# Softmax attention: score parts in two layers of 48 rows, four score banks, three single banks of maxima

## The reference, cut to what matters

```python
q, k, v = (proj(Wq), proj(Wk), proj(Wv))            # 16 heads of 16, of layernorm(x)
q, k = _apply_rope(q, k, cos, sin)
scores = jnp.einsum('bhqd,bhkd->bhqk', q, k) / jnp.sqrt(jnp.float32(dk))
attn = jax.nn.softmax(scores, axis=-1)
out = jnp.einsum('bhqk,bhkd->bhqd', attn, v)
out = out.transpose(0, 2, 1, 3).reshape(B, S, D)
return out @ Wo.T                                    # and x is added
```

## Time and profile before

| | |
|---|---|
| median of 3 runs | 2536.96 us (2531.14 to 2543.85) |
| the profiled execution | 2535.98 us, of which its span 2534.3 us |
| busy over the span | PE 94%, DVE 66%, ACT 52%, POOL 46% |
| the changed stage (`attention_mix`) | about 234 to 1102 us of the span |

### The profile page before, as it was taken

The page is one execution under the profiler, slowest core; times in us unless marked ns, Lnnn a source line. Parts: engine busy times, 40 slices in busy tenths (PEclk is TensorE's granted clock), DMA queues, the critical chain, the costliest instruction groups (busy, mean ns, idle before and its releaser), DMA issues. The chain is left out here.

```text
span 2534.3 us, 48428 instructions
## 1 busy us (share of the span) xinstructions
PE 2376.7 (94%) x14822; PEld 1280.9 (51%) x14822; DVE 1666.4 (66%) x3797; ACT 1328.7 (52%) x2742; POOL 1154.1 (46%) x1497
## 2 busy tenths in 40 slices
PE   8997999999999999979998996999999969998997
PEld 5663233333333333346656664566666646655765
DVE  6777888888888888547763333677777757764332
ACT  5666676667776676645433333455555525432322
POOL 7998111111111111124326775677777734325776
PEclk9998799999999999989998998999999989998999
DMA  6655433323232322136767884011111025685886
GB/s 190 218 188 164 122 87 96 93 88 100 76 106 80 104 84 84 34 96 211 262 225 202 226 210 81 14 39 39 35 39 37 18 72 186 203 299 166 230 221 109
DMA packets 286870, 325.20 MB, mean 128 GB/s; under 512 B 30496, under 2 KB 272368, under 8 KB 286704
## 3 DMA queue, kind: packets, MB, share of 16 engines
q1 hardware_dynamic: 252928, 274.22, 34.7%
q0 software_dynamic: 29184, 46.43, 9.0%
q10 hardware_dynamic: 4592, 2.47, 0.4%
HBM read 217.29 MB, written 105.19 MB: 127 GB/s over the span
## 5 line engine op out<-in xcount | busy, mean ns | idle before, releaser
L718 DVE TENSOR_REDUCE a_row_max<-a_ps_m 128x2 f32<-128x1024 f32 x512 | 607.6, 1219 | 85.0 <-PE a_ps_m L621 80.1
L778 ACT ACTIVATE a_probs<-a_ps_s 128x512 f32<-128x512 f32 x1024 | 536.9, 602 | 207.6 <-PE a_ps_s L649 207.3
L664 PE MATMUL a_ps_o<-a_probs,a_va 128*32 128x512 f32 x2048 | 274.1, 608 | 0.8 <-ACT a_o_sb L787 0.8
L1758 POOL TENSOR_TENSOR b_spread<-b_decay,held_own_sb 128x512 f32<-128x512 f32 x256 | 267.7, 1077 | 8.6 <-DVE b_weight L1819 8.6
L1819 DVE TENSOR_TENSOR b_weight<-b_ps_s,b_spread 128x512 f32<-128x512 f32 x256 | 163.7, 682 | 9.4 <-PE b_ps_s L1960 9.4
L649 PE MATMUL a_ps_s<-first_qs,first_ks 98*128 98x512 bf16 (+1 forms) x512 | 161.3, 396 | 3.5 <-DMA first_qs<-a_m_parts 3.5
L649 PE MATMUL a_ps_s<-second 98*128 98x512 bf16 (+1 forms) x512 | 156.9, 386 | 4.4 <-DMA second<-a_m_parts 2.4
L558 POOL CAST a_high<-a_row_max 128x32 bf16<-128x32 f32 x32 | 6.5, 204 | 316.8 <-DVE a_row_max L718 316.8
L599 POOL DMA_DIRECT2D x<-a_xo x32 | 24.2, 755 | 275.1 <-DVE a_xo L752 272.6
L317 PE MATMUL a_ps_qk<-a_w_qk,a_xnT 128*128 128x512 f32 x256 | 122.2, 600 | 0.0
L1568 DVE SCALAR_TENSOR_TENSOR m2e_h<-m2e_act_g,m2e_xg,m2e_ps_h 128x192 f32<-128x192 f32 x64 | 26.5, 415 | 138.1 <-ACT m2e_act_g L1497 138.1
(11 more groups left out here) (397 smaller groups left out, 5397.0 us busy)
## 6 DMA issues: line engine op xcount, KB each, us to landing
parts<-second SPq DMA_DIRECT2D x16, 1536.0 KB, 6.2
second<-parts SPq DMA_DIRECT2D x384, 64.0 KB, 2.2
rows<-m_early SPq DMA_DIRECT2D x32, 640.0 KB, 3.7
m_early<-x SPq DMA_DIRECT2D x31, 512.0 KB, 4.0
first_qs<-parts SPq DMA_DIRECT2D x192, 64.0 KB, 2.4
first_ks<-parts SPq DMA_DIRECT2D x192, 64.0 KB, 2.2
m_own<-in_L_ffn_w_gate_dram SPq DMA_DIRECT2D x24, 384.0 KB, 4.5
m_own<-in_L_ffn_w_up_dram SPq DMA_DIRECT2D x24, 384.0 KB, 5.2
```

The costliest lines, as they stand in the source:

```text
L664: last = nc.tensor.matmul(ps_o[VW * j:VW * (j + 1), :], va[n.u][:, t, (h0 + j) * VW:(h0 + j + 1) * VW], probs[:, group % 2, j, t, :], star ...
L718: nc.vector.tensor_reduce(row_max[:, n.k // 4 % 2, t, :, n.p % 4], m_bank(name, step)[:], AX.X, ALU.max).then_inc(m_drained, 1)
L778: nc.scalar.activation(probs[:, group % 2, j, t, :], s_bank(name, step)[:], ACT.Exp, scale=DK ** -0.5).then_inc(s_drained, 1)
L1758: nc.gpsimd.tensor_tensor(spread[:, n % 2, heads].rearrange("p h t c -> p (h t) c"), decay[:, n % 3, heads].rearrange("p h (t o) -> p (h t ...
```

## The change

The six blocks are no longer stacked in one contraction of 96 rows. `qs` and `ks` now hold two layers: layer 0 has blocks 0 to 2 (those of the maximum product) and layer 1 blocks 3 to 5 with the two rows of -1 and of the maximum behind them. In each layer e = 0 has the rows from 0 on and e = 1 those from 64 on (`EDGE`). A score is now two matmuls that add up in one bank, of 48 and of 50 rows, and those of e = 0 and 1 alternate, so that every score product has the shape of the maximum products. `scores(t)` makes both heads' scores of key tile t: four matmuls, two banks, and its wait is for both banks at once; it stands four times in a step instead of eight. `ps_m` becomes a ring of three single banks with a turn of its own for every product, and a TENSOR_REDUCE takes 512 columns, one head; `ps_s` becomes a ring of four banks. `exponentials(i)` now serves head i % 2 and tile i // 2. TensorE's order in a step is new: max0, scores 0, scores 1, max1, turn_output, mix (lag 8), turn_shift, max2, scores 2, scores 3, max3, turning, projection, mix (lag 7). ScalarE's order is not changed: `copy_output` is still third.

```diff
-ROW = ((0, 16, 32, 48, 64, 80), (64, 80, 96, 0, 16, 32))
+LAYERS = 2
+EDGE = 64
...
-                row = ROW[e][slot]
-                yield tile[row:row + 16, f * 8 + e:(f + 1) * 8:2, :], src[e]
+                row = EDGE * e + slot % MAX_SLOTS * 16
+                yield tile[row:row + 16, f * 4:(f + 1) * 4, slot // MAX_SLOTS, :], src[e]
...
-    M_RING, S_RING = 2, 3
-    M_ORDER = [("max0", 0, 1, 0), ("output", L_OTURN, 2, 1), ("shift", L_TURN, 4, 3), ("max1", 0, 1, 0), ("max2", 0, 1, 0), ("max3", 0, 1, 0),
-               ("out0", L_OUT[0], PAIRS, PAIRS - 1), ("out1", L_OUT[1], PAIRS, PAIRS - 1)]
+    M_RING, S_RING = 3, 4
+    M_ORDER = ([(f"max{i}", 0, 1, 0) for i in range(4)] + [("output", L_OTURN, 2, 1), ("shift", L_TURN, 4, 3)]
+               + [(f"max{i}", 0, 1, 0) for i in range(4, 8)] + [(f"out{q}", L_OUT[q], PAIRS, PAIRS - 1) for q in range(2)])
...
-        ps_m = [pb(f"ps_m{u}", [P, 2, S]) for u in range(M_RING)]
+        ps_m = [pb(f"ps_m{u}", [P, S]) for u in range(M_RING)]
...
-            nc.gpsimd.memset(ks[0][32:64, 1::2, :], -1.0).then_inc(rows_set[0], 1)
-            nc.gpsimd.memset(qs[0][32:64, 1::2, :], 0.0).then_inc(rows_set[0], 1)
-            nc.gpsimd.memset(ks[0][96:98, 0::2, :], -1.0).then_inc(rows_set[0], 1)
+            for e in range(2):
+                at = slice(EDGE * e + FILL_ROW, EDGE * (e + 1))
+                nc.gpsimd.memset(ks[0][at, :, 1, :], -1.0).then_inc(rows_set[0], 1)
...
-                    name = f"max{t}"
-                    wait(pe, m_drained, m_turn(name, step) + 1 - M_RING)
+                    names = [f"max{2 * t + e}" for e in range(2)]
+                    wait(pe, m_drained, m_turn(names[1], step) + 1 - M_RING)
                     for e in range(2):
-                        rows = slice(ROW[e][0], ROW[e][0] + MAX_SLOTS * DK)
-                        last = nc.tensor.matmul(m_bank(name, step)[:, e, :], qs[u][rows, 2 * n.p + e, t * P:(t + 1) * P], ks[u][rows, 2 * n.p + e, :],
-                                                start=True, stop=True)
-                    last.then_inc(m_filled, 1)
+                        rows = slice(EDGE * e, EDGE * e + PART_ROWS)
+                        nc.tensor.matmul(m_bank(names[e], step)[:], qs[u][rows, n.p, 0, t * P:(t + 1) * P], ks[u][rows, n.p, 0, :],
+                                         start=True, stop=True).then_inc(m_filled, 1)
...
-                    name = f"score{i}"
-                    wait(pe, s_drained, s_turn(name, step) + 1 - S_RING)
-                    h = 2 * n.p + e
-                    nc.tensor.matmul(s_bank(name, step)[:], ks[u][0:K_ALL[e], h, t * P:(t + 1) * P], qs[u][0:K_ALL[e], h, :],
-                                     start=True, stop=True).then_inc(s_filled, 1)
+                    names = [f"score{2 * t + e}" for e in range(2)]
+                    wait(pe, s_drained, s_turn(names[1], step) + 1 - S_RING)
+                    for layer, shift_rows in ((0, 0), (1, 2)):
+                        for e in range(2):
+                            rows = slice(EDGE * e, EDGE * e + PART_ROWS + shift_rows)
+                            last = nc.tensor.matmul(s_bank(names[e], step)[:], ks[u][rows, n.p, layer, t * P:(t + 1) * P], qs[u][rows, n.p, layer, :],
+                                                    start=layer == 0, stop=layer == 1)
+                            if layer == 1:
+                                last.then_inc(s_filled, 1)
...
-            walk_pairs(pe, [(0, max_products(0)), (L_S, scores(0)), (L_S, scores(1)), (L_OTURN, turn_output), (L_MIX + 1, mix_values(1)),
-                            (L_TURN, turn_shift), (0, max_products(1)), (L_S, scores(2)), (L_S, scores(3)), (0, max_products(2)), (L_S, scores(4)), (L_S, scores(5)), (L_MIX, mix_values(0)),
-                            (0, max_products(3)), (L_S, scores(6)), (L_S, scores(7)),
-                            (L_ATT[0], turn_att(0)), (L_ATT[1], turn_att(1)), (L_OUT[0], project(0)), (L_OUT[1], project(1))])
+            walk_pairs(pe, [(0, max_products(0)), (L_S, scores(0)), (L_S, scores(1)), (0, max_products(1)),
+                            (L_OTURN, turn_output), (L_MIX + 1, mix_values(1)), (L_TURN, turn_shift),
+                            (0, max_products(2)), (L_S, scores(2)), (L_S, scores(3)), (0, max_products(3)),
+                            (L_ATT[0], turn_att(0)), (L_ATT[1], turn_att(1)), (L_OUT[0], project(0)), (L_OUT[1], project(1)), (L_MIX, mix_values(0))])
...
-                    name = f"max{t}"
-                    dve.wait_ge(m_filled, m_turn(name, step) + 1)
-                    nc.vector.tensor_reduce(row_max[:, n.k // 4 % 2, t, :, n.p % 4], m_bank(name, step)[:], AX.X, ALU.max).then_inc(m_drained, 1)
+                    for e in range(2):
+                        name = f"max{2 * t + e}"
+                        dve.wait_ge(m_filled, m_turn(name, step) + 1)
+                        nc.vector.tensor_reduce(row_max[:, n.k // 4 % 2, t, e, n.p % 4:n.p % 4 + 1], m_bank(name, step)[:], AX.X, ALU.max).then_inc(m_drained, 1)
...
-                    group, j, t = n.k // 2, 2 * (n.k % 2) + i // QT, i % QT
+                    group, j, t = n.k // 2, 2 * (n.k % 2) + i % 2, i // 2
```

More of the change, by code:

```diff
@@ L384, in attention_mix @@
         woT = sb("woT", [P, 2, D])
-        fill = sb("fill", [P, 2])
+        fill = sb("fill", [P, 1])
         ident, wo_rows = const["ident_sb"], const["wo_rows"]
-        qs = [const["first_qs"], const["second"][:, 0:H * S].rearrange("p (h t) -> p h t", h=H)]
-        ks = [const["first_ks"], const["second"][:, H * S:].rearrange("p (h t) -> p h t", h=H)]
+        qs = [const["first_qs"], const["second"][:, 0:H * S].rearrange("p (g l t) -> p g l t", g=PAIRS, l=LAYERS)]
+        ks = [const["first_ks"], const["second"][:, H * S:].rearrange("p (g l t) -> p g l t", g=PAIRS, l=LAYERS)]
         vs = sb("vs", [P, QT, D])
@@ L536, in heads_of @@
                 return va[u][:].rearrange("p t (h w) -> p t h w", w=VW)
-            for k, value in enumerate((-1.0, 0.0)):
-                nc.gpsimd.memset(fill[:, k:k + 1], value).then_inc(fill_set, 1)
-            pool.wait_ge(fill_set, 2)
-            nc.gpsimd.memset(ks[0][32:64, 1::2, :], -1.0).then_inc(rows_set[0], 1)
-            nc.gpsimd.memset(qs[0][32:64, 1::2, :], 0.0).then_inc(rows_set[0], 1)
-            nc.gpsimd.memset(ks[0][96:98, 0::2, :], -1.0).then_inc(rows_set[0], 1)
-            pool.wait_ge(rows_set[0], 3)
+            nc.gpsimd.memset(fill[:], -1.0).then_inc(fill_set, 1)
+            pool.wait_ge(fill_set, 1)
+            for e in range(2):
+                at = slice(EDGE * e + FILL_ROW, EDGE * (e + 1))
+                nc.gpsimd.memset(ks[0][at, :, 1, :], -1.0).then_inc(rows_set[0], 1)
+            pool.wait_ge(rows_set[0], 2)
             for u in range(2):
@@ L632, in turn_shift, with scores @@
                 for t in range(QT):
-                    last = nc.tensor.transpose(bank[0:2 * HALF, 0, t * P:(t + 1) * P], high_low[:, t].rearrange("p e r g -> p (e r g)"), ident[:])
+                    last = nc.tensor.transpose(bank[0:2 * HALF, t * P:(t + 1) * P], high_low[:, t].rearrange("p e r g -> p (e r g)"), ident[:])
                 last.then_inc(m_filled, 1)
-            def scores(i):
+            def scores(t):
                 def stage(n, step):
-                    u, e, t = n.u, i // QT, i % QT
-                    if n.p % 4 == 0 and i == 0:
+                    u = n.u
+                    if n.p % 4 == 0 and t == 0:
                         f = n.p // 4
                         pe.wait_ge(rest_loaded[u][f], 16 * 4 * (len(Q_PARTS) - MAX_SLOTS) * (n.base + n.k // PERIOD + 1))
-                        pe.wait_ge(rows_set[u], 3)
+                        pe.wait_ge(rows_set[u], 2)
                         pe.wait_ge(w_copied, 1)
@@ L676, in turn_output @@
                 for t in range(QT):
-                    last = nc.tensor.transpose(bank[:, 0, t * P:(t + 1) * P], o_sb[:, group % 2, t * P:(t + 1) * P], ident[:])
+                    last = nc.tensor.transpose(bank[:, t * P:(t + 1) * P], o_sb[:, group % 2, t * P:(t + 1) * P], ident[:])
                 last.then_inc(m_filled, 1)
@@ L727, in copy_shift @@
                 wait(dve, m_odd_loaded[f], n.base * 64 + n.k // PAIRS * 32)
[L728 removed]
+                nc.vector.tensor_copy(m_parts[:, f, :], m_bank("shift", step)[0:2 * HALF, :]).then_inc(m_drained, 1)
             def normalise(n, step):
@@ L750, in stage @@
                     wait(dve, stored[q], n.base * 32 + n.k // PAIRS * 16)
-                    out = m_bank(f"out{q}", step)[:, 0, :].rearrange("p (t d) -> p t d", d=D)
+                    out = m_bank(f"out{q}", step)[:].rearrange("p (t d) -> p t d", d=D)
                     nc.vector.tensor_tensor(xo[:, q], out, xr[n.u][:, 2 * q:2 * q + 2, :], ALU.add).then_inc(m_drained, 1)
                 return stage
-            walk_pairs(dve, [(0, maxima(0)), (L_OTURN, normalise), (L_TURN, copy_shift), (0, maxima(1)), (0, maxima(2)), (0, maxima(3)),
```

(13 more changed lines are left out.)

29 lines of the change are left out of this document (13 added, 16 removed).

## The result

The changed kernel takes 2598.01 us (median of 4 runs, 2590.73 to 2602.92) against 2536.89 before: a ratio of 1.0239 (95% interval 1.0219 to 1.0260), slower. Forecast were 2577 and slower with a chance of 0.82; the time lies in the range, 21 us above the forecast. The span of the profiled execution grew by 59.4 us, from 2534.3 to 2593.7.

What follows compares the result with a forecast made beforehand. TensorE, busy 99 of 100 us at full clock, was taken as the bound. Odd steps +61, even steps -22 and the start +5 and -3 gave +41 on 2536.0: 2577 us, eight-in-ten range 2532 to 2625.

Steps and rivals of the forecast that it cites:

- The shape changes removed: TensorE: six of ten changes of shape a step go, sets 0.225 us apart; natural even step 4.90 us, 0.54 less.
- Rival 2: TensorE: side-by-side pairs lose 0.10 us each time; even steps 5.84, odd 7.35, total 2644 us; chance 0.07.
- The wait that comes in: Odd steps: the last scores(t) waits for exponential 3, queued behind the copy; stall 1.2 us, odd step 7.01 against 6.01.
- Rival 1: Odd steps: the wait for exponentials 2 and 3 does not bite; odd step 5.81, total 2504 us; chance 0.11.
- rival 4: Odd steps: half of the wait is hidden, 0.6 instead of 1.2 us; +4, total 2540 us; chance 0.06.
- Reductions: VectorE: 512-column reductions 0.61 us apart, 0.68 long; second M not before 1.16, so an even step is 4.96.
- Turning and projection: Steps 1 to 4: one more change of shape, 0.1 us each, between M and a mix; projection stays 1.83.
- The start: First steps at half clock: M pairs every 1.38 us instead of 1.12, +5; next four steps gain 0.8 each, -3.
- Rival 3: Attention stage: new pauses make the clock fall; 2603 us if one in four does, 2680 if all; chance 0.10.
- The sum: Whole kernel: odd steps +61, even steps -22, start +5 and -3; in all +41 us on 2536.0.
- The two weighed rules of the Trainium skill: VectorE's 120-cycle fixed cost: even steps 5.27, sum some 7 us longer; 26 ns per increment on TensorE: some 4 us.

Runs made afterwards that it cites:

- e5: e1 with the layers undone: each score again one product of 98 or 112 stacked rows, rings, orders and reductions kept; 2555.32 us, ratio to before 1.0069.
- e1: Changed kernel with the copy of ps_o moved on ScalarE from behind exponential 1 to behind exponential 3; 2532.15 us, ratio to before 0.9991.
- e2: Changed kernel with turn_output moved on TensorE behind the mix of lag 8, ScalarE's order kept; 2547.15 us, ratio to before 1.0047.
- e3: e1 with the mix of lag 7 moved ahead of turning and projection on TensorE; 2534.25 us, ratio to before 0.9994.
- e7: e1 with turn_shift moved ahead of the mix of lag 8 on TensorE; 2520.73 us, ratio to before 0.9936.
- e6: e1 with each TENSOR_REDUCE reading 256 of its 512 columns, so maxima of half the keys; 2492.61 us, ratio to before 0.9825.

## Why the prediction came out as it did, point by point

- **The shape changes removed.** Right. Pairs follow each other 0.22 apart at full clock too, which no row had shown; plain even steps are 4.98 (4.96 forecast), and e5 brings the loss back where it was worked out. Rival 2 is refuted with it.
- **The wait that comes in.** Right, and shown from both ends: e1 takes the exponentials from behind the copy (-66 us, -67 expected), e2 takes 0.9 us from the wait for the mix (-51, -49 expected). Plain odd steps 6.95, forecast 7.01. Rival 1 (the wait does not bite) is refuted. Of rival 4 (half hidden) nothing showed.
- **Reductions.** Pitch and duration right: two consecutive ones take 1.29, one of them 0.68, so they are 0.61 apart:

```profile
721.32 1.29 DVE L720 TENSOR_REDUCE a_row_max<-a_ps_m 128x1 f32<-128x512 f32 x2 [0.25 <-PE a_ps_m L619]
```

  The second M starts at 1.17 to 1.18 (718.71 - 717.54), forecast 1.16.
- **Turning and projection: the largest miss of the sum.** I wrote "0.1 each" and let the projection itself stay. It stands behind an M now, in the ring of three banks, and I worked out the bank wait for turn_output but not for it:

```profile
686.58 0.39 PE L619 MATMUL a_ps_m<-first_ks,first_qs 48*128 48x512 bf16 x2
687.17 2.00 PE L704 MATMUL a_ps_m<-a_woT,a_attT 128*128 128x256 f32 x8 [0.20 <-DVE a_row_max L720]
689.10 1.06 PE L665 MATMUL a_ps_o<-a_probs,a_va 128*32 128x512 f32 x8
```

  0.59 from M to the projection, where M to another shape takes 0.31, and 1.93 for the projection instead of 1.83. The 0.28 is the bank wait (e3 removes it there). The 0.10 is not the change from projection to mix: in e3 an M follows the projection, as before the change, and it takes 1.93 there too (556.54 to 558.47). It lies at the projection's first product. The single starts in the trace have the second product 0.32 behind the first (687.17 to 687.49), before the change 0.22 (604.35 to 604.57), when a score of 112 rows stood ahead of the projection; why the first product costs more now is not shown. The extra change of shape itself was in the forecast's 0.4 for step 2 but not in its 0.2 for step 4. Together steps 2 and 4 came out 0.36 and 0.43 above the forecast, 12 us over 15 sequences.
- **The load of the maxima: not in the forecast.** I looked at what waits on TensorE, VectorE and ScalarE, and wrote of the DMAs that they keep number and sizes. They keep their latency too: from the end of the cast to the first scores that need the load go 2.93 us in the changed kernel. Before, 3.1 us lay between the two and nothing waited (M to score is 0.32 in step 1). The time between them shrank in two ways. Step 0 got 0.36 shorter, and turn_shift stands 2.49 us behind the first M of its step instead of 2.02, because two more scores and an M now stand ahead of the mix in front of it. In step 1 of the changed kernel:

```profile
675.95 1.05 PE L648 MATMUL a_ps_s<-second 48*128 48x512 bf16 x8 [0.57 <-DMA second<-a_m_parts]
```

  The scores start 0.96 behind their M instead of 0.23; a part of that comes back behind them, where turn_output no longer waits for its bank. Step 1 came out 0.4 above step 3, which is built alike and has no such load ahead of it: 6 us over 15 sequences. e7, which issues the load earlier, takes 0.32 off step 1.
- **The start.** Five steps with M alone: 1.39 a pair, forecast 1.38. The next four were to gain 0.8 each and did not: steps 5 to 7 took 8.40, 7.04 and 8.06 against 7.53, 6.03 and 7.89. The first mix comes only at the end of step 7, so that the last M of a half step and the first of the next stand side by side, and the second waits for VectorE, which the row from such a step shows:

```profile
271.36 0.61 PE L619 MATMUL a_ps_m<-first_ks,first_qs 48*128 48x512 bf16 x2 [0.79 <-DVE a_row_max L720]
```

  The start cost 6.4 us, forecast 2. The clock went to the 2.4 GHz level at 280.4 us before and at 287.3 after, both times a few us behind the start of the first mix (276.3 and 284.6), so that the longer start ran at the low level throughout.
- **The clock.** Rival 3 did not come: 1.00 in the stage, with a pause of 1.02 us in every odd step. Longer pauses can be followed by a fall, as the load of the maxima shows, which in a few sequences takes longer than 2.93 us. In e1, with the clock (1.00 or 0.51, ahead of the DMA share) of the stretch behind:

```profile
1004.05 1.05 PE L648 MATMUL a_ps_s<-first_qs,first_ks 48*128 48x512 bf16 x8 [1.59 <-DMA first_qs<-a_m_parts]
...
1005.00:1008.00 3.00, 3.00 (x16) 0.92 (x12) 1.88 (x4) 1.76 (x4) 0.00 (x0) 0.51 0.00 0
```

  And in the changed kernel, where a pause as long left the clock as it was:

```profile
1065.00 1.05 PE L648 MATMUL a_ps_s<-first_qs,first_ks 48*128 48x512 bf16 x8 [1.62 <-DMA first_qs<-a_m_parts]
...
1066.00:1069.00 3.00, 2.61 (x22) 0.79 (x18) 2.67 (x6) 1.73 (x5) 0.00 (x0) 1.00 0.00 0
```

- **The sum.** +41 forecast, +59 measured: 12 from the projection, 6 from the load, 4 from the start, and about -4 from plain odd steps a little shorter than forecast and from roundings.
- **The two weighed rules of the Trainium skill.** The fixed cost of 120 cycles that the Trainium skill states ("VectorE: DVE Perf Modes", section "The TRN2 errata — SBUF-src ops pay a fixed extra latency per instruction") would, as an estimate, have made plain even steps 5.27; they are 4.98, so by the trace the pitch of 0.61 holds. Of the cost of an increment in the Trainium skill's "TensorE: Matmul & The Clock Gate", section "The cost: per-tile semaphore tail", nothing shows, but no run tests it. M to its reduction is 0.42 in e3 (551.55 to 551.97, by its timeline) and was 0.43 with one increment, yet this reduction waits for the first of the two increments alone, and the one that waits for the second starts 0.61 later, behind it.

## What to carry to other kernels

When buffers are regrouped so that more work runs ahead of a point on one engine, the order on the engines behind it has to move along: a copy that waits for that point must not stand ahead of the consumers of the work that now comes earlier. An interval-by-interval sum of the full engine plus the chain of one added wait gave each plain step here to 1%; what it missed were mainly the rarer steps and the start, so every user of a shrunken ring, and every transfer whose cover got shorter, needs its own line. A wait that disappears is to be looked for in the next step too (e3).

## What the runs showed of the hardware

- Changing from side-by-side products of 48 rows to products over more rows or to 32-column ones, and back, costs 0.09 to 0.10 us each time. M to stacked scores is 0.32 (e5) and to scores of its own shape 0.23; in a mix the second pass starts 0.45 behind the first (714.05 to 714.51), and the M starts 0.55 behind the second (715.05), by the single starts in the trace.
- Side-by-side pairs behind each other cost 0.22 a pair of 512 columns at the 2.4 GHz level, with no increment on a pair or with two.
- From the end of the cast to the first scores behind the load of the maxima go 2.93 or 2.94 us in the changed kernel, e1, e6 and e7, whatever stands between them on TensorE.
- Near the stage's start TensorE was busy 5.00 of 5 us and stayed at the 1.2 GHz level, yet in the changed kernel, busy 88% with a pause of 1 us in every other step, it stayed at the 2.4 GHz level. Pauses behind the load were followed by a fall to the 1.2 GHz level at 1004.05 in e1 (1.59 us idle), 394.55 in e5 (1.88) and 430.80 and 966.73 in e6 (1.79 and 1.86), and not at 1065.00 in the changed kernel, 393.57 in e2 and 392.12 in e3 (1.62 each). The length of a pause alone does not decide it, and no run told what does.
